# Linear attention and a Mamba block on one core: dt's low-rank input and B, C as partial sums in column groups, ScalarE's moves one slot later

## The reference

```python
xm, z = split(h @ W_in)                    # 512 channels each, h the modulated norm, in the order perm
xm = silu(causal_conv4(xm) + conv_b)
xdbl = xm @ W_xp                           # 512 -> 64 + 16 + 16
dtr, Bm, Cm = split(xdbl)
dt = softplus(dtr @ W_dt + b_dt)
for step t:
    h = h * exp(dt_t * A) + (dt_t * x_t) * B_t     # 512 channels x 16 states
    y_t = sum over the states of h * C_t
y = (y + xm * D_param) * silu(z);  out = x + gate * (y @ W_out)
```

## Time and profile before

| | |
|---|---|
| runs | 2333.40, 2334.24, 2334.27 us (median 2334.24) |
| the profiled execution | 2334.89 us, its span 2333.1 us |
| PE busy | 2051.4 us, 88% |
| DVE busy | 1969.4 us, 84% |
| ACT busy | 1688.3 us, 72% |
| POOL busy | 1635.2 us, 70% |
| mean granted clock of PE | 0.965 |

### The profile page before, as it was taken

How to read it: one execution, slowest core, us unless ns; L and a number is a source line. 1 busy time by engine, 2 the same in 40 slices (tenths; PEclk the granted TensorE clock), 3 DMA queues, 4 the chain that set the end, 5 groups by cost and what they waited for, 6 DMA issues and landing times. The chain is left out here.

```text
span 2333.1 us, 44474 instructions
## 1 busy us (share of the span) xinstructions
PE 2051.4 (88%) x13497; PEld 1579.0 (68%) x13497; DVE 1969.4 (84%) x3686; ACT 1688.3 (72%) x3652; POOL 1635.2 (70%) x1800
## 2 busy tenths in 40 slices
PE   4899999995699999999999999999999999999870
PEld 3566666662467777777777777777777778777760
DVE  2788888884299898989889898989989898988983
ACT  0455555552688888898888879898888979888840
POOL 2799999985667676776767677776767677676530
PEclk8999999996699999999999999999999999999995
DMA  5122212211000000000000000000000000000218
GB/s 142 39 64 64 64 62 63 62 49 36 10 1 19 6 15 6 15 15 6 15 5 19 6 15 8 13 15 6 20 6 15 6 15 15 6 6 6 95 69 288
DMA packets 71471, 80.75 MB, mean 35 GB/s; under 512 B 12227, under 2 KB 63619, under 8 KB 69188
## 3 DMA queue, kind: packets, MB, share of 16 engines
q1 hardware_dynamic: 66052, 69.52, 9.3%
q10 hardware_dynamic: 5184, 8.39, 1.0%
HBM read 44.33 MB, written 33.55 MB: 33 GB/s over the span
## 5 line engine op out<-in xcount | busy, mean ns | idle before, releaser
L632 ACT ACTIVATE decay<-dtT,decay_rate 128x256 f32<-128x256 f32 x2048 | 866.5, 495 | 0.2
L527 PE MATMUL bank<-ident,decay 128*128 128x128 f32 x4096 | 622.4, 275 | 101.6 <-ACT decay L632 56.0
L537 PEld LDWEIGHTS bank<-ident,scaled 128*128 128x128 f32 x4096 | 486.2, 142 | 231.6 <-issue 193.1
L537 PE MATMUL bank<-ident,scaled 128*128 128x128 f32 x4096 | 622.8, 275 | 1.5 <-POOL scaled L452 1.4
L527 PEld LDWEIGHTS bank<-ident,decay 128*128 128x128 f32 x4096 | 471.7, 141 | 143.7 <-ACT decay L632 103.7
L452 POOL TENSOR_SCALAR scaled<-state,bc 128x512 f32<-128x512 f32 x384 | 278.2, 730 | 255.9 <-DVE state L752 209.3
L742 DVE TENSOR_TENSOR bank<-bank,state 128x512 f32<-128x512 f32 x512 | 340.8, 691 | 117.7 <-PE bank L527 111.5
L452 POOL TENSOR_SCALAR scaled<-fresh,bc 128x512 f32<-128x512 f32 x384 | 273.5, 717 | 235.0 <-DVE fresh L752 214.3
L742 DVE TENSOR_TENSOR bank<-bank,fresh 128x512 f32<-128x512 f32 x512 | 340.3, 690 | 58.9 <-PE bank L527 55.4
L752 DVE SCALAR_TENSOR_TENSOR fresh<-dtx,bc,bank 128x512 f32<-128x512 f32 x512 | 356.9, 737 | 0.0
L752 DVE SCALAR_TENSOR_TENSOR state<-dtx,bc,bank 128x512 f32<-128x512 f32 x512 | 356.8, 737 | 0.0
(11 more groups left out here) (139 smaller groups left out, 3617.0 us busy)
## 6 DMA issues: line engine op xcount, KB each, us to landing
xt<-in_x_dram SPq DMA_DIRECT2D x64, 128.0 KB, 2.2
resid<-x SPq DMA_DIRECT2D x64, 128.0 KB, 1.8
normed<-xh SPq DMA_DIRECT2D x64, 128.0 KB, 1.7
xg<-normed SPq DMA_DIRECT2D x64, 128.0 KB, 2.1
ssm_out<-yo SPq DMA_DIRECT2D x32, 256.0 KB, 2.0
fin_r<-resid SPq DMA_DIRECT2D x8, 1024.0 KB, 13.2
mask_bc<-in_mask_BxS_ik_dram SPq DMA_DIRECT2D x64, 64.0 KB, 2.9
fin_y<-ssm_out SPq DMA_DIRECT2D x32, 128.0 KB, 3.0
```

The source lines that it names most:

```text
L527: mm = pe.transpose(dec_bank[i % DECAY_BANKS][:, m * P:(m + 1) * P], decay[:, i // BLOCK % 2, n % GROUP, m, t % HALF * P:(t % HALF + 1) * ...
L537: mm = pe.matmul(y_bank[t % HALF][:, m * P:(m + 1) * P], scaled[:, i % RING, m * P:(m + 1) * P], ident[:, :], is_transpose=True, start=Fal ...
L632: act.activation(decay[:, block % 2, e // CB, m, :], dtT[par][:, m, half * HTOK:(half + 1) * HTOK], ACT.Exp, scale=decay_rate[:, m, n:n + ...
```

## The change

- dtr: the four products of 128 rows x 64 columns went to the same 64 partitions of the bank, in four slots. Now two slots (23 and 25) hold two products each: one to partitions 0 to 63, one to 64 to 127, so that the bank holds two partial sums. ACT moves all 128 partitions to `dtrT`. W_dt is loaded twice, one copy below the other (`w_dt` is 128 x 512, by one more DMA), so that dt's products add up the two halves over 128 rows in place of 64.
- B and C: a new job bcT (slots 26 and 27) makes four partial sums of 32 rows each, one of each channel block, in four column groups of one bank, by products of 128 x 32 with 512 moving columns. ACT moves them to `bcT`. The job bc (slots 36 and 37) is then one product for each step, with `bcT` as the weights and `eye_sum` (four identities of 32, made once by VectorE) as 32 moving columns; it turns and adds the groups.
- Slots: dt0 to dt3 come one slot later (28, 30, 32, 34), POOL's softplus begins at slot 39.
- `MOVE_LAG` = 2: every move of ACT stands two slots after the job's last PE slot, where it stood one slot after it, and so do the logarithm (now in slot 37, before in 35) and the tanh of z.

```diff
+MOVE_LAG = 2
-        w_dt = sb("w_dt", [DTR, DI])
+        w_dt = sb("w_dt", [P, DI])
+        eye_sum = sb("eye_sum", [P, 2 * DS])
-        dtrT = sb("dtrT", [DTR, TOK], ssm_mem)
+        dtrT = sb("dtrT", [P, TOK], ssm_mem)
+        bcT = sb("bcT", [P, TOK], ssm_mem)
-                "dtr dt0 dt1 dt2 dt3 bc out0 x0 x1 x2 x3").split()
+                "dtr bcT dt0 dt1 dt2 dt3 bc out0 x0 x1 x2 x3").split()
-                                (22, 23, 24, 25), (27,), (29,), (31,), (33,), (35, 36, 37, 38),
+                                (23, 25), (26, 27), (28,), (30,), (32,), (34,), (36, 37),
-        MODULATE, CARRY, SOFTPLUS, GATES = (28, 33), 24, 38, 56
+        MODULATE, CARRY, SOFTPLUS, GATES = (28, 33), 24, 39, 56
...
                 elif kind == "dtr":
-                    pe.wait_ge(s_xs, (c + 1) * CB + piece + 1)
-                    m = X_ORDER[piece]
-                    mm = pe.matmul(side[0:DTR, :], w_xp[:, m, 0:DTR], xs[1 - par][:, m, :],
-                                   start=(piece == 0), stop=(piece == CB - 1))
+                    pe.wait_ge(s_xs, (c + 1) * CB + 2 * piece + 2)
+                    for g in range(P // DTR):
+                        m = X_ORDER[2 * piece + g]
+                        mm = pe.matmul(side[g * DTR:(g + 1) * DTR, :], w_xp[:, m, 0:DTR], xs[1 - par][:, m, :],
+                                       start=(piece == 0), stop=(piece == pieces - 1), skip_group_check=True)
+                elif kind == "bcT":
+                    for g in (2 * piece, 2 * piece + 1):
+                        mm = pe.matmul(side[g * 2 * DS:(g + 1) * 2 * DS, :], w_xp[:, g, DTR:DTR + 2 * DS],
+                                       xs[1 - par][:, g, :], start=True, stop=True, tile_position=(0, g * 2 * DS))
                 elif kind == "bc":
-                    t = piece
-                    for m in range(CB):
-                        mm = pe.matmul(side[:, t * 2 * DS:(t + 1) * 2 * DS], xs[1 - par][:, m, t * P:(t + 1) * P],
-                                       w_xp[:, m, DTR:DTR + 2 * DS], start=(m == 0), stop=(m == CB - 1))
+                    if piece == 0:
+                        moved(pe, c, "bcT")
+                    for t in (2 * piece, 2 * piece + 1):
+                        mm = pe.matmul(side[:, t * 2 * DS:(t + 1) * 2 * DS], bcT[:, t * P:(t + 1) * P], eye_sum[:, :],
+                                       start=True, stop=True)
...
-                    ins = act.activation(dtrT[:, :], side[0:DTR, :], ACT.Copy)
+                    ins = act.activation(dtrT[:, :], side[:, :], ACT.Copy)
+                elif kind == "bcT":
+                    ins = act.activation(bcT[:, :], side[:, :], ACT.Copy)
...
-                        if SLOTS[job][-1] + 1 == i and job[:3] != "out" and runs(job, post, scan, pre):
+                        if SLOTS[job][-1] + MOVE_LAG == i and job[:3] != "out" and runs(job, post, scan, pre):
...
-                    if pre and i == SLOTS["dt3"][-1] + 2:
+                    if pre and i == SLOTS["dt3"][-1] + 1 + MOVE_LAG:
...
-                    if pre and i == SLOTS["x3"][-1] + 1:
+                    if pre and i == SLOTS["x3"][-1] + MOVE_LAG:
...
+            ve.tensor_reduce(eye_sum[:, :], ident[:, :].rearrange("p (g e) -> p e g", e=2 * DS), AX.X, ALU.add)\
+                .then_inc(s_step, 1)
...
-                    sp.dma_start(w_dt[:, :], W_dt).then_inc(s_ssm_w, 16)
+                    for g in range(P // DTR):
+                        sp.dma_start(w_dt[g * DTR:(g + 1) * DTR, :], W_dt).then_inc(s_ssm_w, 16)
```

More of the change, by code:

```diff
@@ L621, in mamba_scalar @@
             attention_over(act)
-            act.wait_ge(s_ssm_w, 16 * 6)
+            act.wait_ge(s_ssm_w, 16 * 7)
             act.activation(decay_rate[:, :, :], decay_rate[:, :, :], ACT.Exp).then_inc(s_prep_a, 1)
@@ L720, in mamba_vector @@
             attention_over(ve)
-            ve.wait_ge(s_ssm_w, 16 * 6)
+            ve.wait_ge(s_ssm_w, 16 * 7)
             ve.tensor_scalar(w_xp[:, :, 0:DTR], w_xp[:, :, 0:DTR], 0.5, None, ALU.mult).then_inc(s_step, 1)
@@ L732, in mamba_vector @@
             ve.memset(state[:, :, :], 0.0).then_inc(s_step, 1)
-            ve.wait_ge(s_step, 19 + 9)
+            ve.wait_ge(s_step, 19 + 10)
             ve.sem_inc(s_prep, 1)
```

## The result

| | before | after |
|---|---|---|
| median | 2333.82 us | 2364.61 us (2363.46 to 2368.75) |
| ratio | | 1.0136, 95% interval 1.0118 to 1.0153 |
| span of the profiled execution | 2333.1 us | 2367.0 us |
| mean granted clock of PE | 0.965 | 0.945 |

What follows compares the result with a forecast made beforehand. No engine bounds it throughout: the path runs h1's move, PE, ACT, PE, DVE, ACT. Terms 0.80 - 1.44 = -0.64 us a chunk, x 15 = -9.6 us, take 2334.24 to 2325 us; range 2312 to 2350.

Steps and rivals of the forecast that it cites:

- step 5: ACT from dt0's move to slot 39: decays done during its wait bring slot 39 and PE's slot 41 by -1.44 us.
- 1. h1's move: Change of chunk: h1's move comes one slot later, so u0 starts 0.80 us later a chunk, with nothing hiding it.
- 2. and 3.: Slots of dtr in pairs and of bcT: each price taken as 1.17 us, between 1.15 and 2.01.
- P: What a slot with two dtr products costs beyond the empty slot, taken as 1.17 us.
- Q: What a bcT slot with two products of 32 columns costs beyond the empty slot, taken as 1.17 us.
- Rival B: Half of each column-group pair overlaps: 1.58 us each, +1.0 us a chunk, 2349 us in all; chance 0.13.
- rival C: No overlap in the column-group pairs: 2.01 us each, +2.7 us a chunk, 2375 us in all; chance 0.06.
- 4. dt0: Counted from the start of slot 22, dt0 comes 0.76 us later, 11.43 us in place of 10.67.
- 6. x0: After slot 45, x0 waits 1.3 to 2.2 us for POOL, ending between 1432.7 and 1433.7; hidden, some 0.7 us cover.
- 7.: One-time costs: second W_dt DMA, reduction for eye_sum and two-part start of the first chunk, taken as 0.
- Formula and path: A chunk changes by 2(P + Q) - 5.32 us; path: h1's move, PE to dt0, ACT to slot 39, PE, DVE, ACT.

Runs made afterwards that it cites:

- experiment 1: Changed kernel plus four unused 128 x 512 products in PE's slot 40, in the wait before slot 41: 2327.83 us, ratio 0.9967.
- experiment 5: Kernel before plus six unused ACT activations of 512 columns ahead of the logarithm in each chunk of the scan: 2414.51 us, ratio 1.0341.
- 8: Changed kernel plus four unused 128 x 512 products in slots 57, 59, 61 and 63, outside the wait: 2366.48 us, ratio 1.0132.
- 7: Kernel before, no column groups, all moves two slots behind except h0's and h1's at one: 2315.73 us, ratio 0.9910.
- 10: Changed kernel plus four unused products in the wait before slot 41, h0 and h1 moved one slot behind: 2314.77 us, ratio 0.9912.
- experiment 3: Changed kernel with MOVE_LAG = 1, so column groups with the old moves: 2353.71 us, ratio 1.0076.
- 11: Kernel before, moves two slots behind except h and x at one, out0 in slots 39-41, x0-x3 in 51, 52, 54, 55: 2317.25 us, ratio 0.9922.
- 9: Changed kernel, out0 in slots 38-40, x0-x3 in 51, 52, 54, 55, h and x moves one slot behind: 2285.46 us, ratio 0.9789.
- experiment 2: Changed kernel with the moves of h0 and h1 back at one slot behind, others at two: 2347.17 us, ratio 1.0049.

## Why the prediction was wrong

The step that failed is **step 5**, or rather what the sum left out behind it: PE's wait before slot 41 was foreseen ("longer, 4 us and more") and priced at nothing. It measures +2.45 us in the chunk shown and +2.56 on average, 38 us in all, and turned -9.6 into a loss. The wait was no idle time to be ignored, since PE is the engine on the path in slots 41 to 45. Experiments 1, 5 and 8 show the cause from three sides: occupied, the wait costs nothing; made long without the change, it costs; and the same work outside it doesn't help. In the scan of the kernel before no repeated wait of PE is longer than 1.56 us (one of 2.43 stands in the first chunk alone), the clock is full, and so no row of the scan priced a wait three times as long. But rows ahead of the scan, while the first chunk is prepared, do show the fall, and the prediction doesn't use them (kernel before; two stretches of busy time, then PE's first turn):

```profile
578.00:584.00 6.00, 2.79 (x6) 0.74 (x6) 3.48 (x3) 2.22 (x4) 5.54 (x5) 1.00 0.00 0
585.00:625.00 40.00, 23.83 (x79) 16.11 (x78) 3.31 (x5) 24.39 (x42) 20.93 (x16) 0.50 0.00 0
...
619.15 1.11 PE L527 MATMUL bank<-ident,decay 128*128 128x128 f32 x4 [5.50 <-ACT decay L632]
```

The clock falls just behind a wait of PE of 2.34 us (its end is at 584.28) and is at half for the next 40 us, over waits of 8.93 and 5.50 us; four transposes take 1.11 us there. With PE on the path for the 7.01 us behind slot 41, this called for a bound of up to some 7 us a chunk (an estimate from these rows: the whole stretch at twice its length), and I gave none. The Trainium skill ("TensorE: Matmul & The Clock Gate", part 1, "HAM oscillation") says that a gap in PE's work brings the clock back to half, and that such a gap in a loop is paid at every turn. The trace agrees: once a chunk, 15 times. I had taken another rule of that page as the one that speaks against this change.

The other steps, by number:

1. h1's move: +0.80 predicted, +0.81 measured, and 0.80 back in experiments 7 and 10 (1446.42 again with a wait of 0.65).
2. and 3. P = 1.18 and Q = 1.13 where I took 1.17 for both. Two column groups run side by side also with 512 columns and in groups of 32. Rival B, one half of each pair overlapped, would have cost 1.58, and rival C 2.01. The Trainium skill's rule of strict program order ("TensorE: Matmul & The Clock Gate", part 3, "What overlaps and what doesn't"), by which I had B, is not what these rows show.
4. dt0 +0.71, predicted +0.76.
5. Slot 41 -1.50, predicted -1.44.
6. x0 waits 1.07 us, where 1.3 to 2.2 were predicted. The slow stretch is not the reason: with a full clock (experiment 1) the wait is 1.09. POOL ends its last product 43.0 us after slot 22 there, 0.2 before the range that I gave for it. In the changed kernel POOL is late together with PE, since its scaled states wait for DVE (1.88 us for one of them in the slow stretch). The end of the chunk is not later for x0's wait: the stretch from slot 45 to 50 is 0.5 us longer and the one from there to the end 0.5 shorter. Hidden.
7. Nothing here that I could tell from the differences between runs of one kernel.

Formula and path were right, then; with the clock held, the change is -0.33% (experiment 1), against the -0.41% that I had summed. The forecast failed in sign by one missing term, what PE's products cost at half clock behind a wait that I had foreseen.

What each part of the change is worth comes out of the table. With the late moves, the groups add nothing by themselves: 7 and 10 differ by 1 us, one without and one with column groups. There they shorten PE's work before slot 41 where ACT is the bound, and so only lengthen PE's wait. With the old moves they bring slot 40 forward by 0.7 us (experiment 3); no run has that with the clock held. They pay when that time is given to other work of PE that stands on the path: out0 moved there is worth nothing without them (11 against 7), and the same order of jobs with and without them differs by 1.3% (9 against 11: 0.9789 and 0.9922).

## What to carry to other kernels

When an edit frees time on TensorE, say what fills it. The waits of 4.4 to 5.4 us on PE in this loop cost not the wait but the half clock behind it, 1.5 to 2.6 us each, and whether that is paid depends on who is on the path right there; price it, even if PE is idle for want of another engine. The repair is to move work from behind the wait into it, and a few products of no use are a fast test of whether that will pay.

## What the runs showed that I had not expected

- In the scan, PE's clock fell in or just behind the waits of 4.42, 4.80 and 5.39 us in every chunk, behind that of 2.61 us in 9 of 15, and at one of 2.44 us that stands once, in the first chunk, in 6 of the 13 traces. It never fell at those of 1.56 us (before) or 1.83 us (experiment 9, before slot 50). Ahead of the scan, where PE has more gaps, it fell in a shorter one too (1.41 us, at 520 us of the kernel before). For the waits of 2.4 to 2.6 us, then, one trace without a fall proves nothing.
- The same wait has no fixed price. Behind 4.43 us in experiment 2 the clock stayed at half for 2.8 to 6.0 us, and slots 41 to 45 took 8.4 to 9.9; behind 4.42 in the changed kernel it was 4.9 to 5.4 us, and 9.41 to 9.65. The mean price is 2.56 us behind 4.42, 1.8 behind 4.80 and 1.5 behind 5.39, so the longer wait is not the dearer one: more of the time at half clock lies in the wait itself, 3.1 us in the chunk shown of experiment 5 and 1.8 in that of the changed kernel.
- The width of a column group hardly matters to what a pair costs: 1.18 us for two of 64 columns and 1.13 for two of 32, each with 512 moving columns.
